# Cross-attention's output projection from slot 5 of the last step on, its preparation three slots apart, its matmuls three to a slot

## What is computed

```python
x = x + _L0_attn_ref(_layernorm(x), ...)
x = x + _L0_xattn_ref(_layernorm(x), ctx, mask, Wq, Wk, Wv, Wo)
x = x + _L0_ffn_ref(_layernorm(x), w_gate, w_up, w_down)
...
attn = softmax(q @ k.T * scale)      # 16 heads of 32
out = attn @ v                       # concatenated to width 512
return out @ Wo
```

## Time and profile before

| | us |
|---|---|
| median of three runs | 3476.01 |
| lowest and highest | 3472.17, 3478.5 |
| the profiled execution, its own time | 3473.2 |
| its span, first to last instruction | 3471.5 |
| last step of cross-attention and output projection, slots 480 to the last transposes | about 2331 to 2520 from the span's start |

### The profile page before, as it was taken

One profiled execution on the slowest core, in us unless ns is written; L12 is line 12 of the kernel. 1 busy time (PEld: TensorE's weight loads), 2 busy tenths in 40 slices (PEclk: granted clock), 3 DMA queues, 4 the chain that ended last, 5 costly groups with the idle time before them and its releaser, 6 DMA issues.

```text
span 3471.5 us, 47183 instructions
## 1 busy us (share of the span) xinstructions
PE 3188.9 (92%) x15056; PEld 2499.6 (72%) x15056; DVE 2588.6 (75%) x4071; ACT 2249.9 (65%) x4127; POOL 1095.1 (32%) x1192
## 2 busy tenths in 40 slices
PE   5999999999999999979999999988989999942998
PEld 4878888888888888856666666655768888732887
DVE  5987878787877787757787878877864469888564
ACT  4876767676776767645777777765432256668665
POOL 1233242333333333344565555556500000000000
PEclk9999999999999999989999999999999999975999
DMA  3443444334434443346565665655712268889764
GB/s 122 167 158 121 129 149 125 128 119 155 122 126 133 134 136 125 95 134 119 117 114 106 125 120 115 124 102 171 233 74 111 113 224 298 327 342 407 267 239 177
DMA packets 273029, 555.49 MB, mean 160 GB/s; under 512 B 28025, under 2 KB 105857, under 8 KB 259473
## 3 DMA queue, kind: packets, MB, share of 16 engines
q1 hardware_dynamic: 268560, 544.08, 52.4%
q10 hardware_dynamic: 4224, 8.39, 0.6%
HBM read 322.72 MB, written 162.30 MB: 140 GB/s over the span
## 4 chain that ended last, share of the span: by engine, by line
PE 33%; DVE 9%; DMA 6%; issue 3%; ACT 2%; SPq 1%; POOL 1%; DVEq 0%; POOLq 0%; ACTq 0%
PE gu_acc L2637 7%; PE ca_mx L2551 3%; DMA gu_g<-gate 3%; DVE ca_negm L2127 3%; PE md_acc L2724 3%; PE md_acc L2725 3%; PE ca_pj L2533 3%; PE md_acc L2726 3%; PE ca_ov L2581 2%; PE ca_ov L2582 2%; PE ca_st L2569 2%; PE ca_pj L2522 2%; DVE ca_el L2142 1%; PE ca_ms L2541 1%; DMA gu_w_raw<-in_L_ffn_w_up_dram 1%
## 5 line engine op out<-in xcount | busy, mean ns | idle before, releaser
L915 POOL TENSOR_SCALAR sa_ex<-sa_ex,sa_rs 128x512 f32<-128x512 f32 x512 | 354.9, 693 | 907.8 <-DVE sa_rs L741 907.8
L736 DVE TENSOR_REDUCE sa_nm<-sa_st 128x1 f32<-128x512 f32 x512 | 350.2, 684 | 224.1 <-PE sa_st L1057 220.1
L578 ACT ACTIVATE sa_eh<-sa_tr 128x512 fp32r<-128x512 f32 x512 | 306.2, 598 | 295.1 <-PE sa_tr L1067 293.3
L1008 PE MATMUL sa_pj<-sa_xh,sa_w 128*128 128x512 f32 x1536 | 455.9, 416 | 3.0 <-DVE sa_xl L714 1.5
L2127 DVE TENSOR_REDUCE ca_negm<-ca_mx 128x2 fp32r<-128x1024 f32 x256 | 312.5, 1221 | 99.7 <-PE ca_mx L2551 95.9
L745 DVE TENSOR_TENSOR sa_el<-sa_tr,sa_eh 128x512 fp32r<-128x512 f32 x512 | 351.2, 686 | 40.9 <-ACT sa_eh L578 34.1
L571 ACT ACTIVATE sa_ex<-sa_st,sa_nm 128x512 f32<-128x512 f32 x512 | 350.9, 685 | 43.3 <-DVE sa_nm L736 39.4
L2420 POOL TENSOR_TENSOR ca_el<-ca_ex,ca_eh 128x512 fp32r<-128x512 f32 x256 | 349.2, 1366 | 62.6 <-ACT ca_eh L1916 62.2
L1908 ACT ACTIVATE ca_ex<-ca_st 128x512 f32<-128x512 f32 x512 | 296.1, 585 | 41.4 <-PE ca_st L2569 39.7
L1067 PE MATMUL sa_tr<-top_ident,sa_ex 128*128 128x128 f32 x2048 | 306.9, 272 | 1.8 <-POOL sa_ex L915 1.8
L1067 PEld LDWEIGHTS sa_tr<-top_ident,sa_ex 128*128 128x128 f32 x2048 | 254.3, 140 | 71.0 <-POOL sa_ex L915 4.3
(11 more groups left out here) (309 smaller groups left out, 7566.4 us busy)
## 6 DMA issues: line engine op xcount, KB each, us to landing
sa_w<-w_split SPq DMA_DIRECT2D x56, 1536.0 KB, 7.5
gate<-gu_ev SPq DMA_DIRECT2D x24, 1024.0 KB, 4.4
gu_g<-gate SPq DMA_DIRECT2D x48, 512.0 KB, 6.4
gate<-gu_g SPq DMA_DIRECT2D x48, 512.0 KB, 3.8
up<-gu_ev SPq DMA_DIRECT2D x24, 1024.0 KB, 5.7
md_ab<-gate SPq DMA_DIRECT2D x96, 256.0 KB, 6.5
md_ab<-up SPq DMA_DIRECT2D x96, 256.0 KB, 7.0
md_ab<-gate SPq DMA_DIRECT2D x44, 512.0 KB, 11.9
```

Of the source, the lines that this page charges most:

```text
L578: nc.scalar.activation(eh[:, v % ER], tr[:, v % 2], ACT.Copy).then_inc(act_eh, 1)
L736: nc.vector.tensor_reduce(nm[:, u % U:u % U + 1], st[:, u % 2], AX_X, ALU.max, negate=True).then_inc(dve_mx, 1)
L915: nc.gpsimd.tensor_scalar(ex[:, u % U], ex[:, u % U], rs[:, u % U:u % U + 1], 1.0, ALU.mult, ALU.mult).then_inc(pool_n, 1)
L1008: yield nc.tensor.matmul(pj[:, bank], w[:, n % 2, m, part, k], xx[b % 2][:, k], start=(i == 0 and k == 0), stop=(i == 2 and k == DK - 1))
```

## The change

It does three things. The steps from -9 to -1 are three slots apart (474, 477, ..., 498), the steps from 0 on four apart as before, beginning in slot 501 (it was 510). So steps 0 to 5 are in slots 501, 505, 509, 513, 517 and 521, and OUT_AFTER is 6: two steps more are inside the loop (its last slots are shared with two tiles more), two fewer behind it. And PE's twelve matmuls of a tile are handed out three to a slot by a generator: three in the step's own slot, three in each of the next three. For this PE's `out_work` issues the transposes of tile i - 2 ahead of the product of tile i, in the loop and behind it. ACT's copy of tile 0 and of tile NT = 4 gets a wait each, on the scores of the last steps, since buffers overlap.

```diff
-    OUT_AT, OUT_PITCH = U * (N - 2) - 6, 4
-    OUT_AFTER = FIRST - (OUT_AT - U * N - LA - AV) // OUT_PITCH
+    OUT_AT, PREP_PITCH, OUT_PITCH = U * (N - 2) - 6, 3, 4
+    OUT_FIRST = OUT_AT - FIRST * PREP_PITCH
+    OUT_AFTER = -((OUT_FIRST - U * N - LA - AV) // OUT_PITCH)
...
         def out_slot(G):
-            i = FIRST + (G - OUT_AT) // OUT_PITCH
-            return i if G >= OUT_AT and (G - OUT_AT) % OUT_PITCH == 0 and i < OUT_AFTER else None
+            if OUT_AT <= G < OUT_FIRST:
+                return FIRST + (G - OUT_AT) // PREP_PITCH if (G - OUT_AT) % PREP_PITCH == 0 else None
+            i = (G - OUT_FIRST) // OUT_PITCH
+            return i if G >= OUT_FIRST and (G - OUT_FIRST) % OUT_PITCH == 0 and i < OUT_AFTER else None
...
-                    if j == 0:
-                        e.wait_ge(pe_st, U * N)
+                    if j in (0, NT):
+                        e.wait_ge(pe_st, U * N if j else U * (N - 1))
...
                     last = nc.tensor.matmul(acc(i), l, wo_hi[:, k], start=False, stop=(k == OT - 1))
+                    if k < OT - 1:
+                        yield
                 last.then_inc(pe_acc, 1)
+                yield
...
-                if is_tile(i):
-                    out_product(i)
                 if is_tile(i - 2):
                     out_transposes(i - 2)
-            work = {}
+                if is_tile(i):
+                    work["out"] = out_product(i)
+            work = {"out": iter(())}
...
                 if out_slot(G) is not None:
                     out_work(out_slot(G))
+                next(work["out"], None)
+            for _ in work["out"]:
+                pass
             for i in range(OUT_AFTER, LAST):
                 out_work(i)
+                for _ in work["out"]:
+                    pass
```

## The result

The changed kernel took 3492.92 us (median of 4 runs, 3492.14 to 3496.75), the kernel before 3474.36 us (3472.17 to 3478.5). The ratio is 1.0051, 95% interval 1.0039 to 1.0064: slower by about 18 us. The forecast was 3482.4 us, within 0.2%, and its range ended at 3490. The profiled execution has a span of 3490.4 us against 3471.5 us.

The account below looks back on a forecast made before the run. The prediction took DVE and POOL to pace the loop. Its five terms, +1.4 + 6.6 - 0.9 - 7.2 + 6.5, gave +6.4 us, from 3476.0 to 3482.4 us, with an 8-in-10 range of 3474 to 3490.

Parts of the forecast that it names:

- Term 1: Before the preparation: ACT's conversion of Wo moves one slot earlier, leaving one slot's work more behind its wait, +1.4 us.
- Term 2: Ahead of slot 501: two more preparation steps at 3.3 us each on DVE, +6.6 us; upper bound 8.4.
- Term 3: Slots 501 to 523: split products save PE waiting, transposes wait 0.7 us for `ca_xn`; 39.0 us, -0.9.
- Term 4: Behind the loop, up to tile 7's product: two steps fewer, product at T + 12.0 instead of T + 19.26, -7.2 us.
- T: Time of the loop's last value products, slot 523: 2402.86 us in the kernel before, forecast to move +7.1 to 2410.
- Term 5: Tiles 7 to 31: transposes ahead of the product wait for `ca_xn`, product pairs 8.11 us apart, +6.5 us.
- A: Rival, in and behind the loop: transposes don't hold up PE because `ca_xn` comes earlier; 3473 to 3476 us, chance 0.19.
- B: Rival, in the loop: it swallows the added preparation, Term 2 at 2 us, besides A; 3469 us, chance 0.06.
- C: Rival, ahead of slot 501: the reciprocals' load paces the preparation, +8 us there; 3490 us, chance 0.20.

Follow-up runs that it names:

- e1: Changed kernel with each tile's product ahead of the transposes again behind the loop, as in the kernel before: 3484.2 us, ratio 1.0014.
- e4: Changed kernel's slots, but a tile's twelve matmuls in one row with transposes behind them, in and behind the loop: 3495.2 us, ratio 1.0050.
- e3: Changed kernel with the preparation four slots apart again, step 0 in slot 510: 3481.2 us, ratio 1.0017.
- e5: Changed kernel with preparation four slots apart, split products and transposes first only inside the loop, old order behind it: 3468.7 us, ratio 0.9982.
- e10: Changed kernel with all steps inside the loop one slot later (502, 506, 510): 3481.6 us, ratio 1.0015.
- e12: e10 with the old order, product ahead of transposes, behind the loop: 3471.2 us, ratio 0.9982.
- e2: Kernel before with only the transposes moved ahead of the product in the steps behind the loop: 3487.0 us, ratio 1.0028.
- e13: e5 with every step inside the loop one slot later, step 0 in slot 511: 3476.7 us, ratio 1.0000.

## Why the prediction was wrong

By its own terms, as marks against the kernel before:

- **Term 1** (+1.4): slot 480 was 0.5 us late, and slot 483 nothing (2336.04 against 2336.19). Small and harmless.
- **Term 2** (slot 501 at 2371, 8 us late with term 1): 2372.53, 12.1 us late. The mechanism was there, DVE's work beside POOL's (`ca_wo_lo` 1.78 us instead of 0.68). The sum is beyond the term's bounds (9.9 with term 1), but part of that is scatter: from slot 474 to 501 the same program took 12.3 us more than before in the changed kernel, 9.9 in e1 and 9.2 in e4. What it missed is PE's idle time, which cost the clock, about 3 us. Six of the nine steps also stand in other places of the eight-slot pattern than before; whether that costs anything was not tested by itself. The forecast also set the old slot 501 at 2363, from a spreading that had waited 1.57 us; its value matmul stands at 2360.42.
- **Term 3** (-0.9, 39 us; bounds 36 to 42): this step failed. It took 44.7 us, and 48.5 in e1 with the same loop, both outside its bounds. The term was summed from PE's own work, 6.5 us a step, plus 0.7 us of waiting for `ca_xn`. But PE did not set the pace, and it never waited for `ca_xn` in this stretch: the steps take 7.8 to 8.8 us in a ring of DVE and POOL. Its reading that a split product mends something was right (e3 and e5: the later steps 6.4 to 6.6 us instead of 6.9 to 7.5), but the move from slots of the form 510 to slots of the form 501 cost more (e10: 6.8 us back).
- **Term 4** (-7.2): -8.3. Tile 7's product came at T + 10.95 instead of T + 12.0, since the clock fell 1.3 us ahead of it and so cost tiles 7 and 8 instead, in the next term. The spreading stands at T + 9.54 (forecast 9.64), released by the reciprocals:

```profile
2426.80 0.71 PE L2625 MATMUL ca_pj<-ca_rc,ca_cast_r 8*128 8x512 f32 x1 [3.78 <-DMA ca_rc<-c_rcp]
```

- **Term 5** (+6.5): +8.8. The mechanism was right, and so was its size in the plain steps: pairs of products 8.07 to 8.10 us apart from tile 9 to 17 (forecast 8.11), the last 7.62 (7.58). The rest is two things: the pair from tile 7 to 9 took 9.07 us, with the clock at 0.50 up to 2430.3, and four of the five pairs from tile 17 to 27, where DVE and PE also prepare the next stage's weights, took 8.45 to 8.53. This is the idle time that did not exist before:

```profile
2506.82 0.66 PE L2615 MATMUL ca_mx<-top_ident,ca_xn 128*128 128x128 f32 x4 [0.70 <-ACT ca_xn L1980]
2511.17 0.66 PE L2615 MATMUL ca_ms<-top_ident,ca_xn 128*128 128x128 f32 x4 [0.96 <-ACT ca_xn L1980]
2514.89 0.66 PE L2615 MATMUL ca_mx<-top_ident,ca_xn 128*128 128x128 f32 x4 [0.29 <-ACT ca_xn L1980]
```

- **Not in the sum**: +4.4 us in the gate and up stage. They come in at one wait, 2.4 us longer, and at the 2.0 us that the next matmuls lose at half the clock behind it (starts 0.43 us apart instead of 0.23). First the kernel before, then the changed one:

```profile
2992.30 1.21 PE L2637 MATMUL gu_acc<-gu_xh,gu_w_hi 128*128 128x512 f32 x4 [2.53 <-DVE gu_w_lo L2164]
```

```profile
3009.72 2.08 PE L2643 MATMUL gu_acc<-gu_xh,gu_w_hi 128*128 128x512 f32 x4 [4.92 <-DVE gu_w_lo L2167]
```

Over all versions that stage, with the same code, took 541.1 to 546.5 us, and which one gets what follows none of the edits. Why that wait for DVE has another length in each profile stays open.

**The rivals.** A and B are out: the product starts are 4.04 us apart in the plain steps, and the loop swallowed nothing. C's 3490 us was the nearest, for the wrong reason: in the changed kernel PE waits for reciprocals once in slots 480 to 501 (1.33 us, ahead of the clock's second fall), and a third buffer did not help beyond scatter. Its weight should not have been lowered by the figure for a DMA's time, though: the section "Anatomy of one DMA — SWDGE (gpsimd) path" of "DMA: Bandwidth & Descriptors" in the Trainium skill is on DMAs that GpSimd issues, and these loads are SP's. The right case, that the steps' phase against a fixed pattern decides, was in none of them. The chance of 0.42 for "slower" took the sign in, but from the wrong cases.

Worked out from the ratios, the changed kernel is the sum of a gain and two losses of like size: the split 0.18% down (e5 against before), the order behind the loop 0.33% up (e10 against e12), the phase 0.36% up (changed against e10); three slots apart and step 0 eight slots earlier come to nothing (e12 against e5: the ratios are equal). These versions form a chain from one kernel to the other, so that the pieces add up to the measured 0.51% is no test. Taken from pairs outside that chain, the order is 0.28% (e2 against before) and the phase 0.32% (e1 against e12), which makes 0.42%: near it, with each ratio known to about 0.1%.

In short: the prediction had the mechanism of the order behind the loop right and put everything else together at nothing (-0.1 us for terms 1 to 4). The step that failed is term 3. It took PE's own work for the pace of the loop, where the place of POOL's and DVE's steps in the other engines' pattern sets it, 7.8 to 8.8 us a step instead of 6.6 to 7.3.

## What to carry to other kernels

When a table of numbers moves periodic work inside a software pipeline, ask first which place in the other pattern's period it lands on: for each engine, what stands directly ahead of and behind the moved step, and who waits for that. A shift by one slot was worth 11 to 14 us in three pairs here and 6 in a fourth (e13), about twice what the split product gave. When reading profiles of such a loop, compare steps that repeat, not the whole stretch: here the first step scattered by up to 4.5 us and hid how well the others agreed. And keep a consumer as far behind its producer as the producer takes: the transposes moved ahead of a product, onto a result that was not ready yet. Handing out work in small pieces and reordering it are two edits, and only the first was good.

## What the runs showed of the hardware

PE's granted clock fell in the middle of the score loop: to 0.50 from 2341.6 to 2348.4 us behind 2.03 us of idle time, and again from 2355.2 to 2372.3 behind 1.33 us, where PE was busy for 15.61 of 17.1 us. A busy PE at the lower level looks like a bottleneck in every view of busy time; the matmul's length tells it apart (value matmuls 0.63 us instead of 0.40). In the gate and up stage 2.4 us more of a wait made 4.4, since the matmuls behind it started 0.43 us apart instead of 0.23.

In the changed kernel DVE and POOL slow each other down: DVE's subtraction `ca_wo_lo` took 0.69 us alone (at 2329.67) and 1.78 us (at 2338.02) beside POOL's `ca_el`, which took 1.75 us there and 1.28 with DVE idle for most of it (at 2330.86).

A spare buffer did not break the ring of two engines: with four instead of three, POOL's wait for DVE's subtraction went, a wait for DVE's statistics in the same step came in its place, and slots 501 to 523 were 51.0 us long, against 44.7 in the changed kernel and 48.5 in e1.
